# A graph network layer on one core: unused two-column instructions on VectorE and ScalarE, and unused gathers on GpSimd

## What is computed

```python
def _mlp2(h, W1, b1, W2, b2):
    return jax.nn.silu(h @ W1 + b1) @ W2 + b2

h_nodes = _mlp2(x, node_W1, node_b1, node_W2, node_b2)
h_edges = _mlp2(edge_attr, edge_W1, edge_b1, edge_W2, edge_b2)
msg_in = jnp.concatenate([h_nodes[dst], h_nodes[src], h_edges], axis=-1)
msgs = _mlp2(msg_in, msg_W1, msg_b1, msg_W2, msg_b2)
agg_sum = jax.ops.segment_sum(msgs, dst, num_segments=num_nodes)
counts = jax.ops.segment_sum(jnp.ones((msgs.shape[0],), msgs.dtype), dst, num_segments=num_nodes)
agg = agg_sum / jnp.maximum(counts, 1.0)[:, None]
upd = _mlp2(jnp.concatenate([x, agg], axis=-1), upd_W1, upd_b1, upd_W2, upd_b2)
out = x + upd
mu = jnp.mean(out, axis=-1, keepdims=True)
var = jnp.mean(jnp.square(out - mu), axis=-1, keepdims=True)
out = (out - mu) * jax.lax.rsqrt(var + LN_EPS) * ln_g + ln_b
...
x = _layernorm(x + _L0_gnn_ref(x, edge_index, edge_attr_64, L0_gnn_node_W1, ...
```

## Time and profile before

| | us |
|---|---|
| device time, median of 2 runs | 4892.27 (4887.94 to 4896.6) |
| span of the profiled execution | 3612.0 |
| busy in the span: PE, DVE, ACT, POOL | 2874.1, 2737.3, 2994.3, 2674.4 |
| the same as a share | 80%, 76%, 83%, 74% |
| mean granted TensorE clock | 0.748 |

### The profile page before, as it was taken

How to read it: one execution, slowest core, us unless ns; L and a number is a source line. 1 busy time by engine, 2 the same in 40 slices (tenths; PEclk the granted TensorE clock), 3 DMA queues, 4 the chain that set the end, 5 groups by cost and what they waited for, 6 DMA issues and landing times.

```text
span 3612.0 us, 103943 instructions
## 1 busy us (share of the span) xinstructions
PE 2874.1 (80%) x16224; PEld 2219.4 (61%) x16224; DVE 2737.3 (76%) x20847; ACT 2994.3 (83%) x23073; POOL 2674.4 (74%) x2823
## 2 busy tenths in 40 slices
PE   4878888877878878888778888777778878877885
PEld 2666666666666666666666666656665656656664
DVE  4777778778777777777787777787777777877876
ACT  4998888888887888988888888888878888888785
POOL 4777777777777777777777777777777777777773
PEclk7687777677777777777777777777777776677766
DMA  7454444454444454444454444444444444444441
GB/s 225 78 113 100 87 94 100 89 102 96 95 95 86 96 102 90 101 100 88 93 103 85 102 96 95 99 95 87 98 92 99 101 89 96 90 92 102 96 95 43
DMA packets 263059, 350.77 MB, mean 97 GB/s; under 512 B 111714, under 2 KB 199121, under 8 KB 252514
## 3 DMA queue, kind: packets, MB, share of 16 engines
q1 hardware_dynamic: 169792, 246.77, 32.0%
q0 software_dynamic: 90624, 95.15, 14.5%
q10 hardware_dynamic: 1954, 2.14, 0.2%
HBM read 330.78 MB, written 13.01 MB: 95 GB/s over the span
## 4 chain that ended last, share of the span: by engine, by line
POOL 62%; issue 21%; PE 8%; DMA 4%; DVE 4%; DVEq 0%; ACT 0%; SPq 0%; ACTq 0%; POOLq 0%
POOL b_ring L834 62%; DMA b_ring<-b_table,src 4%; PE p_pre L696 2%; PE p_pre L702 1%; DVE colbuf L642 1%; PE p_sum L716 1%; PE p_hid L849 1%; DVE comb L939 1%; DMA work<-in_xT 1%; PE p_pre L705 0%; PE p_last L995 0%; PE p_last L996 0%; DVEq L627 0%; DVE stats L1032 0%; ACT colbuf L642 0%
## 5 line engine op out<-in xcount | busy, mean ns | idle before, releaser
L834 POOL DMA_INDIRECT b_ring<-b_table,src x2800 | 2652.0, 947 | 858.9 <-issue 844.8
L642 ACT COPY colbuf<-shared 64x4 uint8 x21134 | 2127.4, 190 | 159.9 <-issue 148.4
L642 DVE COPY colbuf<-shared 64x4 uint8 x17511 | 1377.6, 194 | 308.6 <-issue 301.9
L696 PE MATMUL p_pre<-wa_ring,comb 128*128 128x64 f32 x6250 | 1047.1, 329 | 0.0
L696 PEld LDWEIGHTS p_pre<-wa_ring,comb 128*128 128x128 f32 x6250 | 996.8, 245 | 0.9 <-issue 0.8
L727 ACT ACTIVATE comb<-p_hid,b_e 64x320 f32<-64x320 f32 x1250 | 652.8, 522 | 360.4 <-PE p_hid L849 350.9
L939 DVE SCALAR_TENSOR_TENSOR comb<-shared,p_const 64x640 f32<-64x640 int32 x625 | 554.0, 887 | 458.8 <-PE p_pre L696 336.2
L716 PEld LDWEIGHTS p_sum<-hot_ring,msg 128*65 128x65 f32 x6250 | 589.2, 181 | 500.0 <-DVE agg L949 265.0
L716 PE MATMUL p_sum<-hot_ring,msg 128*65 128x64 f32 x6250 | 649.5, 269 | 291.1 <-DVE agg L949 166.6
L702 PE MATMUL p_pre<-b_ring,ident 128*128 128x320 f32 (+1 forms) x1250 | 583.4, 559 | 341.4 <-DMA b_ring<-b_table,src 340.8
L849 PE MATMUL p_hid<-e_ring,w_e 128*128 128x320 f32 x1250 | 626.2, 591 | 49.0 <-DMA e_ring<-in_edgeT 40.0
(11 more groups left out here) (106 smaller groups left out, 599.2 us busy)
## 6 DMA issues: line engine op xcount, KB each, us to landing
e_ring<-in_edgeT SPq DMA_DIRECT2D x250, 320.0 KB
shared<-in_dst_row SPq DMA_DIRECT2D x125, 640.0 KB
b_ring<-b_table SPq DMA_DIRECT2D x3200, 0.2 KB
b_ring<-b_table,src POOLq DMA_INDIRECT x2800
e_ring<-in_edgeT SPq DMA_DIRECT2D x50, 400.0 KB
shared<-in_dst_row SPq DMA_DIRECT2D x25, 800.0 KB
wa_ring<-a_table SPq DMA_DIRECT2D x625, 16.0 KB
work<-in_xT SPq DMA_DIRECT2D x25, 250.0 KB
```

The costliest lines, as they stand in the source:

```text
L642: end = copy(colbuf[:, special % COLBUF, at:at + 1].bitcast(U8), of[j])
L696: return eng.matmul(p_pre[:, i % 2, k * H:(k + 1) * H], comb[:, i % COMBS, k * P:(k + 1) * P], wa_ring[:, i % RING, :], start=k == 0, stop ...
L834: eng.indirect_dma_start(b_ring[:, b_slot(i), k, :], None, b_table, bass.IndirectOffsetOnAxis(ap=src[:, u * TILES + k:u * TILES + k + 1], ...
```

## The change

Nothing that the kernel computes or stores for its result is changed. Added are:

- in rounds 2 to 6, 8 to 12 and 14 to 18, VectorE runs `paired_columns` in each unit, behind the copies and ahead of `add_sums`: 12 instructions that each read two single columns of `nT` (two of the addresses just loaded) and write one unused column. The form differs: tensor_tensor in rounds 2 to 6, tensor_scalar with the second column as its pointer in 8 to 12, scalar_tensor_tensor with `iota_p` as pointer in 14 to 18
- in rounds 20 to 23, ScalarE runs `biased_columns` in each unit: three Identity activations of one column with another column as bias
- behind the last real gather, GpSimd runs 72 unused gathers with the indices 0, 1, 2, ... : eight each of nine shapes, and after every eight it waits until they have landed
- one iota at the start, and three tiles for the unused values.

```diff
+PAIRED = {**{r: "tensors" for r in range(2, 7)}, **{r: "pointer" for r in range(8, 13)}, **{r: "masked" for r in range(14, 19)}}
+BIASED = range(20, 24)
...
+    iota_low = sb("iota_low", [P, 1], I32)
+    unused = sb("unused", [P, 8, 16], F32)
+    unused_rows = sb("unused_rows", [P, 8, 2 * H], F32)
+    s_unused = sem("unused_rows_in")
...
+        eng.iota(iota_low[:, :], [[0, 1]], base=0, channel_multiplier=1)
...
+    def paired_columns(eng, how, starts, at):
+
+        ends = [nT_bytes[:, ds(start, 4)].bitcast(F32) for start in starts[0:24]]
+        for j in range(0, 24, 2):
+            if j % 6 == 0:
+                for ap in ends[j:j + 6]:
+                    eng.lower_ap(ap)
+            to = unused[0:H, at, j // 2:j // 2 + 1]
+            if how == "tensors":
+                eng.tensor_tensor(to, ends[j], ends[j + 1], ALU.add)
+            elif how == "pointer":
+                eng.tensor_scalar(to, ends[j], ends[j + 1], None, ALU.add)
+            else:
+                eng.scalar_tensor_tensor(to, ends[j], iota_p[0:H, 0:1], ends[j + 1], ALU.mult, ALU.add)
+
+    def biased_columns(eng, starts, at):
+
+        ends = [nT_bytes[:, ds(start, 4)].bitcast(F32) for start in starts[0:6]]
+        for ap in ends:
+            eng.lower_ap(ap)
+        for j in range(0, 6, 2):
+            eng.activation(unused[0:H, at, 12 + j // 2:13 + j // 2], ends[j], ACT.Identity, bias=ends[j + 1])
...
+    def unused_gathers(eng):
+
+        n = 0
+        for rows, width in ((P, H), (96, H), (H, H), (32, H), (16, H), (P, 2 * H), (P, 32), (P, 16), (P, H)):
+            table = b_table.rearrange("n h -> (n h)").rearrange("(n h) -> n h", h=width)
+            for slot in range(8):
+                eng.indirect_dma_start(unused_rows[0:rows, slot, 0:width], None, table,
+                                       bass.IndirectOffsetOnAxis(ap=iota_low[0:rows, :], axis=0)).then_inc(s_unused, 16)
+                n += 1
+                eng.wait_ge(s_unused, 16 * n) if n % 8 == 0 else None
...
             copied_columns(eng, "scalar", eng.copy, j + LEADIN, starts_a, 1, 2).then_inc(col_ok["scalar"], 1)
+            if i // ROUND in BIASED:
+                biased_columns(eng, starts_a, i % 8)
...
             copied_columns(eng, "vector", eng.tensor_copy, j + LEADIN, starts_v).then_inc(col_ok["vector"], 1)
+            if i // ROUND in PAIRED:
+                paired_columns(eng, PAIRED[i // ROUND], starts_v, i % 8)
             if i >= ADD_LAG:
                 add_sums(i - ADD_LAG)
...
                 pool_gathers(eng, range(EARLY, UNITS))
+                unused_gathers(eng)
```

## The result

| | us |
|---|---|
| before, median of 2 runs | 4892.27 (4887.94 to 4896.6) |
| after, median of 2 runs | 5283.28 (5269.78 to 5296.79) |
| ratio | 1.0814, 95% interval 1.0767 to 1.0861 |
| predicted | 5185, range 5040 to 5400 |

The change costs 391 us. That lies in the range, but the working behind the forecast was sound only in parts, and the first thing to be said is about its base. The rows of the kernel before came from an execution with a span of 3612.0 us, much quicker than any run that was timed; a second profile of the same kernel, taken with the first experiment, has a span of 4893.2, and it is the one to hold against the profile after. There is hardly any time outside the span: the profiled run of that second execution took 4895.1 us, 2 more than its span, and the median after is 15 us above the span of 5268.0.

What follows compares the result with a forecast made beforehand. The prediction took GpSimd's gathers, one every 1.25 us, as the bound. VectorE's part 234 us, ScalarE's 0 and the gather tail 60 made 294 us on 4892.27: 5186, stated as 5185, range 5040 to 5400.

Steps and rivals of the forecast that it cites:

- The base: Whole kernel before: GpSimd's gathers, one every 1.25 us, set 140.3 us a round; profiled span 3612.0 us.
- Rival 4: Time outside the profiled span grows in proportion: 294 x 1.354 = 398 us more, time 5290; chance 10%.
- The register instructions: VectorE's 15 changed rounds: 12 added per unit at 93 ns each, 1.91 us a unit, net 1.51.
- rival 2: VectorE's added register instructions are dearer, 140 ns instead of 93: time 5396; chance of that or above 10%.
- The slack: VectorE's waits for the second layer and destination rows: 17.7 us a round, taken off its added 37.8.
- What the ring gives back: GpSimd's gathers, up to 8 units ahead, absorb 33 us of lag; with 35 from unchanged rounds, 302 becomes 234.
- the free rounds: Unchanged rounds 7 and 13 would win back 17.7 us each of GpSimd's lag.
- Three forms alike: VectorE's three kinds of added instruction cost the same, 1.91 us a unit, since the sequencer needs more than the engine.
- ScalarE: 0: Rounds 20 to 23: 19.5 us a round against 14 of slack, 22 in all, within GpSimd's 33 of lag: 0.
- GpSimd's tail: 72 unused gathers after the last real one: 104 us, less 43.65 of last units and update, +60; bounds +51, +85.
- Rival 3: In ten rounds with two SBUF tensors, VectorE's instructions each hold GpSimd 161 ns: 280 us more, 5465; chance 3%.
- The signs: Expected profile: 93 ns register instructions, changed rounds 160 us, others 140, GpSimd newly waiting some 230 us for pre_mm.

Runs made afterwards that it cites:

- the first experiment: The kernel before, unchanged and profiled again: 4884.1 us beside 4875.5, ratio 1.0004, span 4893.2.

## Why the prediction was right, and where it was wrong

- **The total.** 5185 against 5283. The forecast of slower was right, and so was the kind of cause: VectorE's register instructions and a tail of gathers. Several steps missed, and in part they cancelled, so that the time lies in the range is in part luck. With the measured 168 ns and nothing else changed the same sum gives (60.2 - 17.7) x 15 - 68 + 60 = 630 us and 5522, outside the range.
- **The base.** "A gather every 1.25 us is the pace", 140.3 us a round, was true of the traced execution and of no timed run. There GpSimd idles for 2100 us, and a round is SyncE's, at 190. The 1280.3 us more that "no row shows" should have been taken as a sign that the runs had another bound; they lie inside the rounds. Rival 4, that the rest outside the span scales, had the wrong picture too: there is no such rest.
- **The register instructions.** "I take each as a full one", 93 ns: they take 168. This is rival 2's mechanism, that half of their operations are of kinds no copy has; its 140 was nearer than my 93. With 168 the formula of the prediction gives 12 x 168 + 24 x 33 = 2.81 us, less 0.5 plus 0.1: 2.41 net, 60.2 a round.
- **The slack.** 17.7 us a round was predicted, 33.8 was there. 60.2 - 33.8 = 26.4; measured are 305 / 15 = 20.3, since VectorE also loses some 10 us a round less in hold-ups at its copies and the addition, a term that the sum had not. The prediction's 20.1 is nearly that number by 37.8 - 17.7: two terms, too small by 22 and by 16, which almost cancel. A good figure from two bad ones.
- **What the ring gives back.** 68 us were taken off. Nothing came back: GpSimd wasn't the bound, it waited for TensorE all along, and the free rounds stay at 185 to 189 us. 15 x 20.3 stand in full, 305 and not 234.
- **Three forms alike.** Right with the register instructions in (1050, 1055 and 1056 us). Without them the forms differ by 44 us in five rounds, so it was the sequencer that made them alike, as argued. The engine's part was not small, though. Its paces of 70, 121 and 131 ns lie within the bounds of 70 and 161, yet by themselves the two slower forms cost 46 and 63 us in five rounds.
- **ScalarE: 0.** Right, ratio 1.0019. The Trainium skill (ScalarE: Activation LUTs, What ACT_TABLE_LOAD costs) was cited for 280 ns of such an activation. The trace agrees for its length, 282 ns, and three in 0.66 us are 189 ns apart, near the 187 net.
- **GpSimd's tail.** +60 predicted, +80 (in the changed kernel) to +97 (alone) measured. The length was right (101 against 104). The step that failed is that the 43.65 us of last units and update "hide a part": the dense gathers hold those units up, and most of that work comes behind them.
- **Rival 3, contention on SBUF in ten rounds.** Didn't show: gathers take 947 ns in the median in tensor, pointer and masked rounds alike and before the change, and the pointer rounds, which lack it, are as long as the others. But a contention of another kind was there from the start, in all rounds, and no rival had it.
- **The signs.** VectorE's waits ahead of the one-hot are gone (though the profile names few of their releasers), "issue" at the unused instructions is up by 25 us a round, and the changed rounds are alike: seen. 93 ns, rounds of 160 and 140, the last gather at 3800, and GpSimd waiting for pre_mm as something new: not seen. It waited 1104 us for lines L702 and L705 before, and 1543 after.

## What to carry to other kernels

Put the span of a profile beside the times before anything else, and if they are far apart, don't cost a change against that profile: its bound may not be the bound of the runs. Count the register instructions behind each operand whose address is worked out at run time, by the operations in them; an address that is cut to words costs more than the instruction that uses it. Work that is "behind the end" is only free of side effects if it leaves the other engines' sequencers alone: put pauses between gathers, or start them when the others are done.

## What the runs showed of the hardware

- A register instruction takes 93 ns on VectorE for a byte address, and 168 ns (148 on ScalarE) where the address is cut to words and multiplied up again; with one ahead of each instruction on VectorE three of them and their three instructions take 0.71 us, the sequencer's time and not the engine's 0.45. That the cut is what makes them dear follows from the code; no run took it out alone.
- Unused gathers of 16 to 128 rows take 0.83 to 0.96 us: the number of rows hardly matters. Most land within 2 us, some take up to 6.4.
- Instructions of one column by 64 partitions take 145 ns (tensor_tensor), 197 (tensor_scalar with a pointer) and 205 (scalar_tensor_tensor), but start 70, 121 and 131 ns apart.
- GpSimd's gathers back to back hold up VectorE, ScalarE and SyncE together, by 0.5 to 1.2 us an instruction, whatever they read. With a pause of 2 us between gathers that is nearly gone: from 4800 to 4915 us VectorE has 9.7 us of "issue" at its copies, against 52.3 with 72 back to back and 8.8 in the kernel before. Which shared thing they stand in line for is not settled: no row names it, and the execution of the earlier trace rows had gathers just as dense and copies 70 ns apart. That execution also had a mean granted clock of 0.748, where the others have 0.58 to 0.62; whether that goes with it or follows from the longer idle times was not tried.
